# A graph network's attention layers: from a walk over pairs of edge tiles to a walk over single tiles, with a rearranged set-up

## What is computed

```python
h = (x @ W).reshape(n, HEADS, HID)
a_s = jnp.einsum('nhc,hc->nh', h, att_src)
a_d = jnp.einsum('nhc,hc->nh', h, att_dst)
e = jax.nn.leaky_relu(a_s[src] + a_d[dst], NEG_SLOPE)
m = jax.ops.segment_max(e, dst, num_segments=n)
ex = jnp.exp(e - m[dst])
denom = jax.ops.segment_sum(ex, dst, num_segments=n)
msg = h[src] * (ex / denom[dst])[:, :, None]
out = jax.ops.segment_sum(msg, dst, num_segments=n)
```

## Time and profile before

| | |
|---|---|
| device time, median of 3 executions | 4796.29 us (4795.19 to 4797.39) |
| the profiled execution's own time | 4815.22 us |
| its span, first to last instruction | 4813.4 us |
| mean granted clock of PE | 0.798 of full speed |
| instructions | 56729 |
| HBM | 495.47 MB read, 41.31 MB written |

### The profile page before, as it was taken

How to read it: one execution, slowest core, us unless ns; L and a number is a source line. 1 busy time by engine, 2 the same in 40 slices (tenths; PEclk the granted TensorE clock), 3 DMA queues, 4 the chain that set the end, 5 groups by cost and what they waited for, 6 DMA issues and landing times. The chain is left out here.

```text
span 4813.4 us, 56729 instructions
## 1 busy us (share of the span) xinstructions
PE 3113.4 (65%) x11125; PEld 1890.6 (39%) x11125; DVE 3030.3 (63%) x8020; ACT 2537.1 (53%) x7729; POOL 2820.6 (59%) x2967
## 2 busy tenths in 40 slices
PE   4699999999999883455555555555355555555551
PEld 3344444444444472333333333343233433334341
DVE  7788888888888753455554555557355554555557
ACT  3588888888888642333333333334233333333347
POOL 2366666666666405666666666638666666666652
PEclk8899999999999996777777667777667677776776
DMA  5332323223333244444444444425444444444435
GB/s 161 98 86 85 88 85 87 85 85 87 89 87 87 71 130 138 111 121 123 129 118 128 116 128 128 118 73 154 117 114 128 129 117 129 116 128 125 121 108 162
DMA packets 274567, 540.54 MB, mean 112 GB/s; under 512 B 73156, under 2 KB 161983, under 8 KB 274240
## 3 DMA queue, kind: packets, MB, share of 16 engines
q0 software_dynamic: 134912, 376.36, 28.7%
q1 hardware_dynamic: 132308, 154.29, 10.2%
q10 hardware_dynamic: 7020, 6.40, 0.4%
HBM read 495.47 MB, written 41.31 MB: 112 GB/s over the span
## 5 line engine op out<-in xcount | busy, mean ns | idle before, releaser
L1247 POOL DMA_INDIRECT arena<-h_rows,idx x1856 | 1773.8, 956 | 1108.8 <-issue 507.7
L1382 PE MATMUL ps<-arena,z 128*128 128x264 f32 x3712 | 1357.2, 520 | 316.9 <-DVE arena L1494 188.8
L769 POOL DMA_INDIRECT arena<-y_rows,idx x928 | 910.2, 981 | 692.0 <-ACT arena L800 292.9
L1306 ACT ACTIVATE z<-z 128x256 f32<-128x256 f32 x928 | 378.5, 408 | 1419.3 <-PE ps L1382 692.0
L1502 DVE TENSOR_TENSOR z<-ps,z 128x264 f32 x928 | 396.8, 428 | 1156.4 <-remote 648.7
L1382 PEld LDWEIGHTS ps<-arena,z 128*128 128x128 f32 x3712 | 883.5, 257 | 543.2 <-DVE arena L1494 228.0
L798 ACT ACTIVATE arena<-arena 128x128 f32<-128x128 f32 x2784 | 914.9, 399 | 189.2 <-DVE arena L885 168.1
L840 PE MATMUL ps<-arena 128*128 128x512 f32 x1856 | 905.0, 611 | 39.6 <-DVE z L893 31.4
L1298 ACT ACTIVATE z<-iota,dst_x 128x128 f32<-128x128 f32 x1856 | 642.5, 393 | 26.3
L1494 DVE TENSOR_TENSOR arena<-arena,ps 128x520 f32<-128x520 f32 x928 | 631.2, 685 | 0.0
L840 PEld LDWEIGHTS ps<-arena 128*128 128x128 f32 x1856 | 345.9, 194 | 529.0 <-issue 526.9
(11 more groups left out here) (231 smaller groups left out, 3052.1 us busy)
## 6 DMA issues: line engine op xcount, KB each, us to landing
z<-lo_rows SPq DMA_DIRECT2D x116, 512.0 KB
arena<-h_rows,idx POOLq DMA_INDIRECT x1856
arena<-y_rows,idx POOLq DMA_INDIRECT x928
z<-seg_rows SPq DMA_DIRECT2D x232, 64.0 KB
h_rows<-arena SPq DMA_DIRECT2D x98, 132.0 KB, 1.8
arena<-h_rows SPq DMA_DIRECT2D x98, 132.0 KB, 2.9
arena<-res_rows SPq DMA_DIRECT2D x98, 128.0 KB, 2.8
z<-in_ea_rows SPq DMA_DIRECT2D x464, 8.0 KB
```

The source lines that it names most:

```text
L769: pool.indirect_dma_start(out=ring[:, r, :], out_offset=None, in_=s.y_rows, in_offset=bass.IndirectOffsetOnAxis(ap=rows_of[:, u, n:n + 1], ...
L1247: pool.indirect_dma_start(out=ring[:, u * SCORED + n, :], out_offset=None, in_=h_rows, in_offset=bass.IndirectOffsetOnAxis(ap=s.idx[:, u, ...
L1306: nc.scalar.activation(sel[:, q % SELS, :, :].rearrange("p k n -> p (k n)"), away[:, q % 2, :, :].rearrange("p k n -> p (k n)"), ACT.Relu, ...
L1382: last = t.matmul(ps[:, bank[q % 4], 0:ROW], sel[:, q % SELS, k, :], ring[:, u * SCORED + 2 * q + k, :], start=(k == 0), stop=(k == 1))
```

## The change

Both attention layers walk single slots. A block gets as many slots as it has tiles; with 831 tiles and 49 blocks there are 880 (SINGLES), which make 27 groups of 32 and a last one of 16 (LEFT); `conv_edges` keeps its 928 paired slots. A step of PE, ACT and DVE still covers two slots (selection, messages), but each slot is collected into a bank of its own (slot n into bank n % 4) and added by itself, since the two may belong to different blocks. Block numbers are loaded for eight slots at a time. The waits count slots.

Core of the diff in `gat_edges`, and the function that it calls:

```diff
+SINGLES = (TILES + BLOCKS) // 2 * 2
+SCORED_GROUPS = -(-SINGLES // SCORED)
+LEFT = SINGLES - (SCORED_GROUPS - 1) * SCORED
+def blocks_of_slots(nc, s, eng, engine):
+    def block(slot):
+        first = slot // 8 * 8
+        if first not in held:
+            held.clear()
+            _, held[first] = nc.values_load_multi_w_load_instructions(
+                s.blk[0:1, first:first + 8], engines=(engine,), min_val=0, max_val=BLOCKS - 1,
...
-    ADDS = STEPS_IN + 1
+    ADDS = SCORED + 1
             def gather(g, u):
-                for n in range(SCORED):
+                for n in range(width(g)):
                     if n % 2 == 0 and not peeled(g, 2):
-                        pool_wait(pool, s, agg_ok, (g - 2) * STEPS_IN + n // 2 + 1)
+                        pool_wait(pool, s, agg_ok, (g - 2) * SCORED + n + 2)
...
             def select(g, q):
-                    act.wait_ge(agg_ok, pair - SELS + 1)
+                    act.wait_ge(agg_ok, 2 * (pair - SELS + 1))
...
             def look_up(g, u, q):
-                block = block_of(pair)
                 for k in range(2):
                     n = (2 * q + k) % HALF
+                    block = block_of(g * SCORED + 2 * q + k)
...
             def collect(g, u, q):
-                if not (isinstance(g, int) and g == 0 and q < 4):
-                    pe.wait_ge(z_ok, g * ADDS + 1 + q - 3 if q >= 4 else (g - 1) * ADDS + 1 + q - 3 + STEPS_IN)
                 for k in range(2):
-                    last = t.matmul(ps[:, bank[q % 4], 0:ROW], sel[:, q % SELS, k, :], ring[:, u * SCORED + 2 * q + k, :], start=(k == 0), stop=(k == 1))
-                last.then_inc(agg_ok, 1)
+                    n = 2 * q + k
+                    if not (g == 0 and n < 4):
+                        pe.wait_ge(z_ok, g * ADDS + 1 + n - 3 if n >= 4 else (g - 1) * ADDS + 1 + n - 3 + SCORED)
+                    t.matmul(ps[:, bank[n % 4], 0:ROW], sel[:, q % SELS, k, :], ring[:, u * SCORED + n, :], start=True, stop=True).then_inc(agg_ok, 1)
...
             def group(g, u, final=False):
-                for q in range(STEPS_IN):
-                    if q + 2 < STEPS_IN:
+                steps = width(g) // 2
+                for q in range(steps):
+                    done = (g, 2 * q - 2) if q else (g - 1, SCORED - 2)
+                    if done[0] >= 0:
+                        add(*done)
+                    if q + 2 < steps:
                         message(g, u, q + 2)
+                    if done[0] >= 0:
+                        add(done[0], done[1] + 1)
                     if q == 0:
-                        if not (isinstance(g, int) and g == 0):
-                            add(g - 1, STEPS_IN - 1)
                         rescale(g)
-                    else:
-                        add(g, q - 1)
```

```diff
-            for n in range(GROUP):
-                sp.dma_start(w8[8 * n:8 * n + 8, n // 2, n % 2 * 64:n % 2 * 64 + 64], a["fc_w1"]).then_inc(wt, 16)
...
-            for pair in range(PAIRED):
+            for pair in range(8, PAIRED):
...
-            v.memset(s.w8[:, :], 0.0).then_inc(wz, 1)
             v.memset(w2, 0.0).then_inc(wz, 1)
-            v.memset(s.z[:, 0:BLOCKS * 512], 0.0).then_inc(zero_ok, 1)
-            dve.wait_ge(zero_ok, 1)
+            def zero(block):
+                v.memset(s.z[:, block * 512:(block + 1) * 512], 0.0).then_inc(zero_ok, 1)
...
                     add(pair - 2)
+                if ZEROED + pair < BLOCKS:
+                    zero(ZEROED + pair)
```

279 lines of the change are left out of this document (179 added, 100 removed).

## The result

The changed kernel takes 4724.36 us (median of 6 runs, 4707.01 to 4752.83) against 4794.76 us before (6 runs): a ratio of 0.9842, with a 95% interval of 0.9814 to 0.987. It is faster by 1.6%, and the interval excludes no change; the forecast was 4911, slower by 2.4%. The measured time lies on the other side of no change, near where rival A had put it (4692). That it is inside the stated range (4655 to 5060) is no merit of the forecast: its own range began at 4860, and it was widened so as to hold A. The profiled execution took 4725.12 us with a span of 4723.3 us.

What follows compares the result with a forecast made beforehand. Bound: POOL's gathers and the PE-DVE chain coupled, sharing a group's time. Layers +114, look-ups +8, set-up -7 gave +115 on the profiled 4815.2 us: 4930, or 4911 at the median; own range 4860 to 5000, stated 4655 to 5060.

Steps and rivals of the forecast that it cites:

- rival A: Attention walk: gathers set the pace, added work goes into DVE's waits; period stays 46.8 us, median 4692 or 4648; chance 0.27.
- C1: Time the PE-DVE chain would need for a whole group under gathers: 52.7 us before the change.
- The full groups: Attention groups with all their gathers: period forecast to grow from 46.8 to 50.8 us.
- C1': C1 after the change: 55.7 us, 3 more for exposed loads and a late addition; 52.7 to 60.7 at its ends.
- Without gathers: Group with no gathers under way: 27.8 us plus 8.6 for additions and 1.6 for block-number loads, 38.0.
- Gathers: POOL's gathers in the walk: 48 fewer a layer, 1.25 to 1.46 us apiece, only where they set the pace.
- rival D: Tables don't cut the gathers or the walk isn't 28 groups: 29 rescales, 5013 us; chance 0.03.
- The four banks: Collect banks hold four tiles, not four pairs, so PE runs two pairs ahead: nothing in the sum.
- rival C: Attention walk: two pairs ahead are too few, 55 us a group, 202 us on top, 5113; chance 0.14.
- The set-up: Work ahead of the attention walk, loads, tables and convolution: together -7.4 us, between -25 and +10.
- the -12.4 at the start of the convolution: Loads moved to ACT's queue let SP's second batch of edge scalars land near 183.6 instead of 196.00: -12.4 us.

Runs made afterwards that it cites:

- e12: The e3 kernel with block numbers loaded side by side, two short loads a group instead of two long ones: 4670.31 us, ratio 0.9741.
- e3: The changed kernel with its 880 slots, but collects and additions by pairs as before: 4677.21 us, ratio 0.9741 to the kernel before.
- e8: The changed kernel with block numbers loaded at a stride of two words, as before: 4770.03 us, ratio 0.9939 to the kernel before.
- e4: The changed kernel with one more DVE instruction of 264 columns, on scratch, in each step: 4759.29 us, ratio 0.9884 to the kernel before.
- e5: The changed kernel with two more DVE instructions of 264 columns, on scratch, in each step: 4829.84 us, ratio 1.0028 to the kernel before.
- e19: The changed kernel with every fourth gather left out from group 2 on, 24 a group instead of 32: 4266.75 us, ratio 0.8868.
- e7: The changed kernel with only the first two groups gathered: 4046.47 us, ratio 0.8404 to the kernel before.
- e1: The kernel before with the new attention walk alone, on the old set-up with its paired tables: 4714.93 us, ratio 0.9809.
- e2: The changed kernel with the old attention walk, 928 slots over tables that hold 880, on the new set-up: 4818.66 us, ratio 1.0041.
- e15: The changed kernel with a POOL memset of 192 columns, and a wait for the one before, ahead of each gather: 4753.23 us, ratio 0.9884.
- e9: The changed kernel with each gather from group 2 on fetching half of each row, 528 of 1056 bytes: 4761.83 us, ratio 0.9861.
- e16: The changed kernel with each gather from group 2 on fetching 64 rows instead of 128: 4775.9 us, ratio 0.9952.
- e13: The changed kernel with SP's two broadcast loads a group cut to one partition of 128 from group 1 on: 4761.27 us, ratio 0.986.
- e17: The e3 kernel with the second of each pair's two collecting matmuls left out: 4652.67 us, ratio 0.9676 to the kernel before.
- e18: The changed kernel with every second look-up matmul left out from group 1 on: 4730.91 us, ratio 0.9838 to the kernel before.
- e14: The changed kernel with one signal for the collects of two slots, behind the second: 4741.15 us, ratio 0.9889 to the kernel before.
- e10: The changed kernel with POOL's lead shorter by 8 slots, 56 instead of 64: 4750.75 us, ratio 0.9867 to the kernel before.

## Why the prediction was wrong

**The step that failed is the reading of the bound: that under gathers the PE-DVE chain shares the period with POOL, so that its growth is paid in every full group. With it went the sign.** I had seen two things rightly: a group takes 27.8 us without gathers and 46.7 with them, and POOL pauses while PE's signals come late. From these I concluded that neither side is alone the pace, and wrote a period in which every microsecond more of the PE-DVE chain is paid at 0.24 in the pauses, and every one more of C1 at a half. The formula gave the 46.8 back, but it had one free number, C1, made from that same 46.8; it explained nothing that it wasn't fitted to. The runs show a full group of 46.4 to 46.9 us for chains of 24.4, 26.5, 27.9, 33.5 and 39.3 us (e12, e3, before, after, e8), and 47.1 and 48.15 us with DVE's additional work, at 36.5 and 42.1 us (e4, e5). Up to 33.5 us the chain costs a full group nothing that could be measured, at 36.5 and 39.3 us it costs 0.7 and 0.4, which the scatter doesn't part from nothing, and at 42.1 us 1.7 (1.5 in the second layer). What the period does follow is the count of gathers: 46.4 us with 32, 37.6 with 24, 33.7 with none (after, e19, e7).

**By its terms.** *The full groups*: 50.8 forecast, 46.45 measured; 24 x 4.35 x 2 = 209 us, which is all of the distance between 4911 and 4724 and a little more. Two mistakes went into it. C1' = 55.7, the 3 us for loads ahead of an addition for which PE waits, was priced with loads of 1.83 and 1.93 us that were 0.59; but e8, which has the long loads, shows that even these would have cost no more than some 0.4 us. And the waits of DVE took up the additions altogether. *Without gathers*: 38.0 forecast, 33.5 measured. The additions were worth about what I took, since e3 to after is 26.5 to 33.5 us, 7.0 with loads that became 1.3 shorter (2.4 for 3.7), so some 8 for the 8.6; the loads were +1.6 in my sum and -1.3 in fact. *Gathers*: I wrote that they are worth their time only where they set the pace. Their count does, though not POOL's speed in issuing them: 96 slots fewer brought 1.2 to 1.5 us each, around my two prices (1.25 and 1.46). The tables do what they say, and rival D is out: 28 rescales a layer and 1760 gathers. *The four banks* as tiles rather than pairs (rival C) show no cost in the period; PE waited 94.8 / 24 = 4.0 us a group for an addition, and the full group didn't grow. *The set-up*: -7 forecast. Measured are 5 to 8 us more in `prepare`; the whole is some +16 by the ratios of e1 and the changed kernel, whose intervals overlap, and +18 in e2, which isn't clean. The eight more gathers were put at +5 and cost about 8 at the fifth block (58.65 for 50.5), behind DVE's wait up to 55.93 us, and the -12.4 at the start of the convolution became -4.3 (39.2 for 43.5): the loads of the second batch, at SP's 1.2 us each in my working, were issued beside POOL's gathers and took 2.7 on the average. It looks like the holding back that I had described for PE; that it is the same isn't shown. I had not asked whether SP's queue would be slower there.

**The rule.** The Trainium skill ("Trainium Architecture — The Big Picture", "What this means for kernel authors") says that engine lanes and DMA ports can't contend for SBUF. What I drew from it, that gathers don't slow the chain, came out in its consequence for this change but not as a statement: 33.7 us a group without gathers and 46.45 with them (e7, after). No run here tests the ports, and what the traces show held up are signals, of which the rule doesn't speak.

**What rival A had.** Its number for the layers was -97 us, from a period that stays at 46.8; they gave 98, and some 4 to 6 more behind the last rescales. Part of that is luck in its terms: it had 38 us for both the group with half the gathers and the one without, which took 42.8 and 33.5. On the profiled executions it had 4711 against 4725.1, and `prepare` and `conv_edges` took 14 us more where it had the set-up at 7 less, which is more than that distance. The other 18 us between 4692 and 4724 are none of the kernel: the profiled execution before lay 18.9 us over its median, the one after 0.8. Against it stood POOL's wait for the chain, 7.3 us a group, and this I took for the proof that the chain shares the pace. e15 is the run that disposes of it: make each gather 0.14 us later, and the pauses shrink by about that much (32 x 0.14 = 4.5 us, and 6.3 to 2.0). A wait that gives way like this is slack, even if both engines wait for each other.

**Still open** is what makes 32 gathers take 46.4 us when POOL can issue them in 40.1. It goes by their count (e19). It isn't their bytes (e9), their rows (e16), SP's broadcasts (e13), PE's passes (e17, e18), DVE's work (e4, e8, e12), the number of signals (e14) or PE's clock (e17); a shorter lead may add to it (e10). That POOL goes on within 1.5 us of the last packet of the gathers in flight is so at the long pauses of both kernels, and would give such a period if each round of gathers had to end with a drain. That is argued, not shown: a pause that ends for another reason would see the queue run dry as well, and no run took the holding itself away: that would need a ring of more than 64 slots, which doesn't fit beside the sums, and it wasn't tried. No run gave a version that computes the same and beats the changed kernel beyond the scatter; e1 points to 10 to 16 us in the set-up, but its tables are those of pairs.

## What to carry to other kernels

When two engines wait for each other, don't make a formula that divides the time between them: ask what happens if one of them gets a little slower, and look for a stretch where that already varies. Long waits on the engine that gets the new work (here 18.8 us of 46.7 on DVE) can be room for it even if the other engine waits too; one run with an idle instruction more a step (e4) tells; and a formula with one number fitted to the period that it explains is no evidence for a slope. Put the numbers that a register load fetches side by side, and don't count what other queues issue beside a stream of gathers at the price that it has without one.
